# Expert tiles of 128 rows in the dispatched mixture-of-experts stage of a decoder kernel, and one zeroing transfer

## The reference

```python
logits = x @ Wg                                  # 8 experts
top_vals, top_idx = top_k(logits, 2)
weights = onehot(top_idx) * softmax(top_vals)
for e in range(8):
    u, v = x @ W1[e], x @ W2[e]                  # 256 -> 512
    out += (u * sigmoid(u) * v) @ W3[e] * weights[..., e]   # 512 -> 256
```

## Time and profile before

| | us |
|---|---|
| median of 3 runs | 2129.85 |
| lowest and highest | 2129.36, 2131.46 |
| the profiled execution's own time | 2127.23 |
| its span | 2125.5 |
| TensorE busy in the span | 1411.7 (66%) |
| VectorE busy | 1307.2 (62%) |
| ScalarE busy | 735.5 (35%) |
| GpSimd busy | 649.5 (31%) |

### The profile page before, as it was taken

The page is one execution under the profiler, slowest core; times in us unless marked ns, Lnnn a source line. Parts: engine busy times, 40 slices in busy tenths (PEclk is TensorE's granted clock), DMA queues, the critical chain, the costliest instruction groups (busy, mean ns, idle before and its releaser), DMA issues. The chain is left out here.

```text
span 2125.5 us, 34473 instructions
## 1 busy us (share of the span) xinstructions
PE 1411.7 (66%) x12171; PEld 1028.4 (48%) x12172; DVE 1307.2 (62%) x2172; ACT 735.5 (35%) x1138; POOL 649.5 (31%) x495
## 2 busy tenths in 40 slices
PE   4777566666766530039999972477458886249998
PEld 2555334434444330039999962364236564236665
DVE  4777478888888566315555555623847774764444
ACT  2222334344344311214444430101326677123443
POOL 0111144555445213830000007500627888200000
PEclk9877688889889755569999995555578786559999
DMA  8100100000000003622211215200363321000000
GB/s 287 37 0 0 50 10 11 10 10 0 10 10 0 1 1 124 224 72 60 68 60 60 68 60 177 62 1 1 63 150 62 65 54 17 0 1 21 20 19 21
DMA packets 71217, 104.46 MB, mean 49 GB/s; under 512 B 9058, under 2 KB 58980, under 8 KB 68580
## 3 DMA queue, kind: packets, MB, share of 16 engines
q1 hardware_dynamic: 64996, 86.64, 14.6%
q0 software_dynamic: 6144, 16.79, 2.3%
HBM read 62.08 MB, written 37.22 MB: 47 GB/s over the span
## 5 line engine op out<-in xcount | busy, mean ns | idle before, releaser
L2413 POOL TENSOR_TENSOR q_pl<-q_ex,q_ph 128x512 f16<-128x512 f32 x128 | 146.7, 1159 | 41.7 <-ACT q_ph L2367 41.1
L1175 PE MATMUL r_pS<-r_qm,r_ks 128*128 128x512 f16 x384 | 114.1, 450 | 58.3 <-DVE r_qm L1329 57.2
L1618 POOL DMA_INDIRECT l_XN<-slot_results,slot x32 | 33.3, 1039 | 352.0 <-issue 352.0
L2216 DVE TENSOR_REDUCE q_mx<-q_pS 128x4 f32<-128x512 f32 x128 | 86.7, 685 | 73.2 <-PE q_pS L2144 72.6
L1386 ACT ACTIVATE r_simh<-r_sim 128x1024 f16<-128x1024 f32 x64 | 67.6, 1057 | 158.9 <-DVE r_sim L1268 157.4
L966 PE MATMUL mt_pU<-mt_xh,mw_w 128*128 128x256 f16 x624 | 116.2, 274 | 1.5 <-DVE mt_xl L1054 1.5
L966 PE MATMUL mt_pV<-mt_xh,mw_w 128*128 128x256 f16 x624 | 115.0, 273 | 0.0
L1461 POOL TENSOR_TENSOR r_siml<-r_sim,r_simh 128x1024 f16<-128x1024 f32 x32 | 68.9, 2154 | 139.0 <-ACT r_simh L1386 138.6
L977 PE MATMUL mt_pY<-mw_w,mt_hh 128*128 x624 | 106.4, 273 | 1.0 <-DVE mt_hl L1068 1.0
L2635 DVE TENSOR_TENSOR s_hc<-s_h,s_pC 128x512 f32<-128x512 f32 x64 | 44.0, 688 | 102.0 <-ACT s_h L2604 102.0
L953 PE MATMUL mt_turn<-ident,mt_xin 128*128 128x128 f32 x156 | 23.9, 277 | 118.7 <-DMA mt_xin<-slot_rows 118.7
(11 more groups left out here) (502 smaller groups left out, 4562.3 us busy)
## 6 DMA issues: line engine op xcount, KB each, us to landing
ahead<-in_L_ffn_W SPq DMA_DIRECT2D x12, 1024.0 KB, 5.2
slot_rows<-zeros SPq DMA_DIRECT2D x3, 3328.0 KB, 21.8
mt_xin<-slot_rows SPq DMA_DIRECT2D x39, 256.0 KB, 2.8
slot_results<-mt_yout SPq DMA_DIRECT2D x39, 256.0 KB, 2.2
q_Q<-q_bounce SPq DMA_DIRECT2D x24, 256.0 KB, 6.3
X<-in_x SPq DMA_DIRECT2D x4, 1024.0 KB
r_ctx<-in_ctxT SPq DMA_DIRECT2D x8, 512.0 KB, 3.9
l_Wp<-in_L_attn_Wp SPq DMA_DIRECT2D x1, 4096.0 KB
```

The source lines that it names most:

```text
L1175: last = pe.matmul(pS[dc][:, heads, :], ks[x][:, dc, t], qm[y][:, heads, dc, t], start=(n == 0), stop=(n == 2))
L2216: dve.tensor_reduce(mx[:, at:at + UNIT], pS[n % 2][:, :, :], AX, ALU.max).then_inc(s["taken"], 1)
L2413: pool.tensor_tensor(pl[n % RING][:, :], ex[n % 3][:, :], ph[n % RING][:, :], ALU.subtract)\
```

## The change

`TILE` becomes 128 rows. By the same line `TILES` becomes (8192 + 8 * 127) // 128 = 71, `STEPS` 32 and `BLK` 1. The PSUM tiles of `expert_tiles` would then be half a bank, and are now taken as whole banks of 512 f32 of which the first part is used. `slot_rows` is zeroed in one transfer, as 71 is not divisible by 3. Lines behind 894 move down by 3 (L966 is L969, L977 is L980, L984 is L987, L996 is L999).

```diff
-ZERO_DMAS = 3
+ZERO_DMAS = 1
...
-TILE = 2 * P
+TILE = P
 TILES = (2 * B * S + E * (TILE - 1)) // TILE
 STEPS = B * S // TILE
...
     HALF = HC // 2
     BLK = TILE // P
-    turn = c.ps("turn", [P, DC, TILE])
-    pU, pV = ([c.ps(f"{n}{i}", [P, HALF, TILE]) for i in range(2)] for n in ("pU", "pV"))
-    pY = c.ps("pY", [P, BLK, D])
+    def bank(name, a):
+        return c.ps(name, [P, 512])[:, 0:a * TILE].rearrange("p (a t) -> p a t", a=a)
+
+    turn = bank("turn", DC)
+    pU, pV = ([bank(f"{n}{i}", HALF) for i in range(2)] for n in ("pU", "pV"))
+    pY = c.ps("pY", [P, 512])[:, 0:BLK * D].rearrange("p (a d) -> p a d", a=BLK)
```

## The result

| | before | after |
|---|---|---|
| median, us | 2129.61 | 2307.9 |
| lowest and highest | 2123.91, 2131.46 | 2304.71, 2312.72 |
| profiled execution's own time | 2127.23 | 2304.71 |
| its span | 2125.5 | 2303.0 |

The ratio of the runs is 1.0844, 95% interval 1.0813 to 1.0875: the change makes the kernel 8.4% slower. The forecast was 2321, within 2298 to 2365.

A forecast was written before the change was run, and what follows sets the result against it. TensorE's array bounds the third stage before the change, its sequencer after. Profiled 2127.2 + 190.3 (stage) + 0.7 (routing) = 2318.2 us; with the median 2.6 above the profiled execution, forecast 2321, range 2298 to 2365.

The forecast's parts named there:

- What bounds the kernel now, and what next: Third stage's tiles: TensorE's array at 8.29 us a tile before; its sequencer after, 7.25 us against the array's 4.22.
- The price of a register instruction: On TensorE's sequencer in the third stage: 0.120 us between starts, bounded from 0.112 to 0.127.
- The edges: Start and end of the third stage, outside its steady tiles: 4 us added to 71 x 7.25 us.
- Routing and zeroing: Routing's larger `more` and `passed` operations add 0.7 us; one zeroing transfer instead of three costs nothing.
- The array as the bound: Rival, third stage: sequencer hides its register instructions, stage 303.6 us, a gain of 24.9, time 2106; chance 5%.
- The clock: Rival, third stage: TensorE's clock falls to 1.2 GHz, 8.1 us a tile, time up to 2383; chance 8%.
- The weight loads: Rival, third stage: loads of some 100 ns not hidden behind 128 columns, 6.3 us a tile, some 2253; chance 3%.
- the 81 ns of the Trainium skill: Third stage: alternative price of a 128-column matmul with weight load; 5.42 us a tile, stage 389, time 2191.
- Item 3: TensorE's waits in the third stage: no data wait shows, cost nothing; cover gone only under 3 us a tile.
- its first rival: Third stage: the array stays the bound, faster, time 2106; argued against by the sequencer's sum per tile; chance 5%.

## Why the prediction was right

- **What bounds the kernel now, and what next.** Right in both. The array was the bound before (a constant expert changes nothing with 256 rows), and the sequencer is after (a constant expert takes 198 us off with 128).
- **The price of a register instruction.** Read as 0.120 us from how far apart they start, not from their recorded 32 to 46 ns. In the changed kernel the mean over all tiles is 0.120. The tile: 7.25 forecast, 7.235 measured; 71 tiles, 1.1 us off.
- **The edges.** The one term of the stage that was mis-sized: 4 us forecast, and 512.7 - 71 x 7.235 = -1.0 measured. From the last transposes to the end the stage takes 11.0 us, 3.8 more than a tile; before it was 14.9, 6.6 more than a tile, and this tail was nearly all of the edge that the prediction carried over. Against it, the 70 distances of the transposes sum to 501.7 us, 4.7 less than 70 x 7.235. The first one is 4.24 us, since only the up projections of half 0 stand between the first two transposes, and the next two, 6.37 and 6.70, lie in tiles that are written out, with no loop's end. So the stage gave +184.3 for +190.3.
- **Routing and zeroing.** +0.73 us of operations for 0.7 forecast; zeroing nothing, shown alone. What the prediction doesn't have: routing's first VectorE operation, behind the block that loads its tables, starts 7.4 us after retention's last matmul and not 6.5 as before. It is 7.1 in the three experiments with 128 rows and 6.5 in the six with 256, so 0.6 to 0.9 us come with the change here; the cause was not tried.
- **The rest of the difference.** Forecast +191, measured 178.3 between the medians and 177.5 between the profiled executions. The stage begins 0.5 us later and is 184.3 longer, and what follows it takes 7.3 us less (860.8 before, 853.5 after), though the change doesn't touch it. The normalisation behind the gathers took 90.0 and 87.1 us, one-key attention 281.7 and 279.4; retention, which lies ahead, 514.0 and 510.7. In the traces of the nine experiments the same stages vary without any edit there: retention from 510 to 521 and one-key attention from 280.1 to 284.6. That normalisation took 87 us in all nine, so there it was the profiled execution of before that was long. I take the 7 us as the spread of single executions; what it comes from was not tried, and no term of the prediction had it.
- **The rivals.** The array as the bound (2106) came true only where the instructions were taken away: 2110. The clock did not fall: 1.00 through the stage at 78% busy. The weight loads were hidden: the matmuls in a constant-expert tile start 0.056 us apart. An estimate by the 81 ns of the Trainium skill ("TensorE: Matmul & The Clock Gate", "Back-to-back issue gap") would have made that tile 5.42 us. It takes 4.21, so the trace does not agree.
- **Item 3**, no data waits, was right: TensorE has no such wait in the changed kernel's steady part.
- What was wrong came later, in an expectation: the step "the tile takes the larger of the sequencer's sum and the array's sum" fails near the threshold. It put one more read at nothing (measured: 6.3 us of the stage) and four more at 9.85 us for a tile (measured: 10.08 and some 10.6), since the sequencer's lead ends at 18 matmuls. The prediction argued by the same rule, against its first rival, that the sum over a tile counts and not its order. There it made no difference, as the changed kernel's sequencer has hardly a lead to lose: counted in the same way, 2 matmuls wait at the end of a tile.

## What to carry to other kernels

Before making the tiles of a loop smaller, count what a tile pays that doesn't shrink with it: register instructions, reads of registers from memory, waits and branches on the busiest engine's sequencer. Their price is the distance between their starts in a stretch where nothing holds the sequencer, and it is owed only where the engine's own work per tile is shorter; a busy share of 100% says nothing of how near that point is. And place what the sequencer must do without issuing work where its queue is full, not behind the branch of a loop, and not so soon after such a stretch that the queue hasn't filled again.

## What the runs showed of the hardware that I had not expected

- TensorE's sequencer leads the array by at most 18 matmuls with their weight loads (17 waiting and one just started, at the end of 37 of 38 tiles in each of five traces of 256 rows). Then it's held, and matmuls that cost it next to nothing cost what the array takes for them, 0.109 us each.
- Matmuls between register instructions are almost free to the sequencer: with one, two or five of them in between, two register instructions start mostly 0.11 to 0.12 us apart and now and then 0.14 to 0.16 (kernel before, 1095.9 to 1100.5), while the sequencer isn't held.
- A read of a register from SBUF costs the sequencer 0.65 us with the two instructions that follow it, though its record is 0.30 us long. In the run with one more read the second read starts 0.65 us after the first (1200.73, 1201.37), and the two together fill 1.28 us.
- Idle time put down to issue shows only part of such a loss. It was 105 us where taking the instructions away won 198, since gaps shorter than a matmul's record are covered by the record.
